# Bulk transfers issued from ScalarE's queue, projection inputs prepared one tile further ahead, and a last output tile made in two column halves

## The reference

```python
for l in range(2):                      # W_stack[l]: 512 x 1024
    proj = x @ W_stack[l]
    Wh, Ws = jnp.split(proj, 2, axis=-1)
    a = jax.nn.softmax(Wh @ Ws.T, axis=-1) * adj
    x = jax.nn.leaky_relu(a @ Wh + x, 0.01)
# then, on the normalised x:
xw = jnp.maximum(jnp.sign(x), 0.0) @ jnp.sign(weight).T
x = layernorm(x + jax.nn.relu(adj @ xw))
```

## Time and profile before

| | us |
|---|---|
| runs: median of 3 (lowest, highest) | 2148.17 (2147.42, 2153.5) |
| profiled execution, its own time | 2151.31 |
| its span | 2149.4 |
| PE busy | 2110.1 (98%) |
| DVE busy | 1592.3 (74%) |
| ACT busy | 908.2 (42%) |
| POOL busy | 689.5 (32%) |
| DMA queue q1 (SP's): share of 16 engines | 73.8% |
| DMA queue q10 (ACT's): share of 16 engines | 1.8% |

### The profile page before, as it was taken

One profiled execution on the slowest core, in us unless ns is written; L12 is line 12 of the kernel. 1 busy time (PEld: TensorE's weight loads), 2 busy tenths in 40 slices (PEclk: granted clock), 3 DMA queues, 4 the chain that ended last, 5 costly groups with the idle time before them and its releaser, 6 DMA issues.

```text
span 2149.4 us, 38691 instructions
## 1 busy us (share of the span) xinstructions
PE 2110.1 (98%) x13260; PEld 1295.3 (60%) x13260; DVE 1592.3 (74%) x4057; ACT 908.2 (42%) x2047; POOL 689.5 (32%) x623
## 2 busy tenths in 40 slices
PE   6999999999999999999999999999999999999998
PEld 2456666666666666664446666666666666665444
DVE  7987877788877778876986776776677776767465
ACT  5764344444444444443765344344434443443000
POOL 2853223232223233222863232333323332322000
PEclk9999999999999999999999999999999999999999
DMA  7998878788878687769998987888878978779794
GB/s 216 213 222 155 175 154 164 157 155 161 169 151 166 154 165 159 161 138 236 204 211 183 184 162 165 162 167 172 168 155 171 169 161 181 158 157 220 218 304 133
DMA packets 779526, 380.18 MB, mean 177 GB/s; under 512 B 642880, under 2 KB 701376, under 8 KB 777664
## 3 DMA queue, kind: packets, MB, share of 16 engines
q1 hardware_dynamic: 768512, 341.89, 73.8%
q0 software_dynamic: 3328, 22.16, 7.0%
q10 hardware_dynamic: 7488, 13.63, 1.8%
HBM read 206.24 MB, written 59.11 MB: 123 GB/s over the span
## 4 chain that ended last, share of the span: by engine, by line
PE 91%; DVE 3%; DMA 2%; issue 1%; ACT 1%; SPq 1%; POOL 0%; DVEq 0%; ACTq 0%; POOLq 0%
PE banks L1157 38%; PE banks L1126 31%; PE banks L783 10%; PE banks L1661 7%; PE banks L1135 3%; DMA adj_rows_a<-adj_rows 1%; PE banks L1115 1%; PE banks L605 1%; DVE halves_a L1385 1%; DMA values<-x_rows 0%; DMA probs_t_a<-halves_a 0%; DVE row_a L1340 0%; SPq L1002 0%; DVE adj_low L1453 0%; DVE w_p L725 0%
## 5 line engine op out<-in xcount | busy, mean ns | idle before, releaser
L1157 PE MATMUL banks<-values,probs_t_a 128*128 128x512 f16 x4056 | 961.2, 380 | 7.3 <-DMA probs_t_a<-halves_a 4.2
L1323 POOL TENSOR_TENSOR row_a<-row_a,adj_rows_a 128x512 f32<-128x512 f32 (+1 forms) x364 | 456.7, 1269 | 1163.7 <-ACT row_a L1245 1133.6
L1157 PEld LDWEIGHTS banks<-values,probs_t_a 128*128 128x128 f16 x4056 | 397.3, 98 | 382.2 <-issue 9.6
L1237 ACT ACTIVATE row_a<-banks 128x256 f32<-128x256 f32 x468 | 177.3, 379 | 628.6 <-PE banks L1126 609.1
L1126 PE MATMUL banks<-keys_t,q_even_a 128*128 128x256 f16 x3528 | 430.9, 273 | 1.8 <-DVE peaks_a L1340 1.1
L1385 DVE SCALAR_TENSOR_TENSOR halves_a<-row_a,halves_a 128x512 f16<-128x512 f32 (+1 forms) x364 | 272.5, 749 | 192.1 <-ACT halves_a L1260 189.7
L1126 PEld LDWEIGHTS banks<-keys_t,q_even_a 128*128 128x128 f16 x3528 | 343.8, 98 | 102.5 <-DVE peaks_a L1340 4.9
L1126 PE MATMUL banks<-keys_t,q_odd_a 128*128 128x256 f16 x3024 | 370.0, 273 | 4.4 <-DVE peaks_a L1340 1.8
L1245 ACT ACTIVATE row_a<-row_a,shift_a,scales 128x512 f32<-128x512 f32 (+1 forms) x364 | 281.4, 774 | 174.0 <-DVE shift_a L1375 173.9
L1126 PEld LDWEIGHTS banks<-keys_t,q_odd_a 128*128 128x128 f16 x3024 | 294.3, 98 | 92.1 <-DVE peaks_a L1340 6.0
L1407 DVE SCALAR_TENSOR_TENSOR acc_a<-acc_a,factor_a,banks 128x512 f32<-128x512 f32 x312 | 232.8, 746 | 106.1 <-PE banks L1157 99.3
(11 more groups left out here) (131 smaller groups left out, 1482.7 us busy)
## 6 DMA issues: line engine op xcount, KB each, us to landing
adj_rows_a<-adj_rows SPq DMA_DIRECT2D x312, 256.0 KB, 3.2
adj_t<-adj_blocks POOLq DMA_DIRECT2D x104, 208.0 KB, 3.9
keys_t<-adj_t SPq DMA_DIRECT2D x26, 832.0 KB, 7.9
x_rows_a<-x_rows SPq DMA_DIRECT2D x52, 256.0 KB, 3.6
s_rows<-sum_rows_p SPq DMA_DIRECT2D x24, 512.0 KB, 3.1
values<-x_rows SPq DMA_DIRECT2D x13, 512.0 KB, 5.4
adj_rows_a<-adj_rows SPq DMA_DIRECT2D x52, 128.0 KB, 2.7
x_mid<-x_rows_a SPq DMA_DIRECT2D x26, 256.0 KB, 3.4
```

What stands on the lines that cost most here:

```text
L1157: last = pe.matmul(out_bank(u), probs_t[:, turned_slot(w), u, ph * tiles + j, :], values[:, 4 * step_of(w) + j, vh, :], start=(j == 0 and ...
L1237: act.activation(quarter(w, u, odd), as_quarter(bank(w, SET_A)), ACT.Copy).then_inc(scores_copied, 1)
L1323: pool.tensor_tensor(piece, piece, adj_rows[:, n % ADJ_RING, 0:width(w)], ALU.mult).then_inc(masked, 1)
```

## The change

It has four parts.

1. **Bulk loads change their queue.** `load_x` for layer 1's rows (not its last), the two small transfers for the weights' peak, `gather_low_bits`, the 22 loads of products and the first 8 loads of adjacency tiles are issued by ACT, at the end of its iteration w, where SP issued them at the end of its own.
2. **Five tiles are prepared ahead, not four** (`FILL = 5`). In layer 0 the fifth tile's high half is made after the last squares and its low half inside `scale_layer`; at the layer seam the five high halves are spread over five iterations.
3. **Layer 0's start is put in another order**: ACT takes the squares of tiles 2 and 3 (DVE did), and makes tile 2's high half between the two sides of the weights.
4. **The last output tile** is made in two column halves of 256: 2 x 26 matmuls into two banks, the first half measured while PE makes the second, the output made and stored in two halves, the second by SP.

```diff
-RING, X_RING = 4, 3
+RING, X_RING, FILL = 4, 3, 5
@@ scale_layer(dve)
         dve.reduce_max(facts[:, 5:6], norms2[:], AX_X).then_inc(norm_peak, 1)
+        if layer == 0:
+            x_lo_half(dve, 4)
         dve.wait_ge(norm_all, layer + 1)
@@ project: act_program
             x_hi_half(act, 1)
+            square_rows(2)
+            square_rows(3)
             act.wait_ge(w_scale_ready, layer + 1)
             for side in (0, 1):
                 for c in range(DC):
                     halve_w(c, cols_of(side))
-            x_hi_half(act, 2)
+                if side == 0:
+                    x_hi_half(act, 2)
...
             for t in range(FIRST + 2, T, 2):
                 square_rows(t)
+            x_hi_half(act, 4)
...
-                if 2 * i + RING + two < T:
-                    x_hi_half(act, 2 * i + RING + two)
+                if 2 * i + FILL + two < T:
+                    x_hi_half(act, 2 * i + FILL + two)
@@ attend: sp_program
-            if ahead and piece_windows.get(w - 3, -1) == pieces - 1:
-                ahead["send_w_peak"](sp)
...
-                ending = w - (windows - STEPS)
-                if 2 <= ending < 5:
-                    binary["load_products"](sp, ending - 2)
-                elif ending in (5, 6, 12, 13):
-                    n = (5, 6, 12, 13).index(ending)
-                    binary["load_adj16"](sp, 2 * n)
-                    binary["load_adj16"](sp, 2 * n + 1)
...
-                if 0 <= behind < WIDE:
-                    ahead["load_x"](sp, 2 * behind)
-                    ahead["load_x"](sp, 2 * behind + 1)
@@ attend: act_program, at the end of an iteration
-            if ahead and w == windows:
-                for t in range(RING):
-                    ahead["x_hi_half"](act, t)
+            if ahead and 0 <= w - windows < FILL:
+                ahead["x_hi_half"](act, w - windows)
+            behind = w - (windows - STEPS) - LAG - 1
+            if ahead and 0 <= behind < WIDE:
+                ahead["load_x"](act, 2 * behind)
+                ahead["load_x"](act, 2 * behind + 1)
...
+            ending = w - (windows - STEPS)
+            if last_layer and 2 <= ending < 5:
+                binary["load_products"](act, ending - 2)
+            elif last_layer and ending in (5, 6, 12, 13):
+                n = (5, 6, 12, 13).index(ending)
+                binary["load_adj16"](act, 2 * n)
+                binary["load_adj16"](act, 2 * n + 1)
@@ binary layer: finish_end(t, b), for the last tile
+            for side, summed, count in ((0, half_summed, 1), (1, sums_done, t + 1)):
+                dve.wait_ge(summed, count)
+                links.link(dve.scalar_tensor_tensor(out=work[:, b, parts[side]], in0=end_bank(t, side), scalar=0.0,
+                                                    in1=work[:, b, parts[side]], op0=ALU.max, op1=ALU.add))
+                links.link(dve.bn_stats(end_stats[:, side], work[:, b, parts[side]]))
...
+            for side, done in ((0, end_half_done), (1, rows_done)):
+                dve.tensor_scalar(y_rows[:, b, parts[side]], work[:, b, parts[side]], stats[:, b, 6:7], std[:, b, 2:3],
+                                  ALU.subtract, ALU.mult).then_inc(done, 1)
```

More of the change, by code:

```diff
@@ L1094, in sp_program @@
                     store(t)
[L1095 to L1096 removed]
+                if 0 <= w - windows < RING:
                     ahead["turn_x"](sp, w - windows)
[L1098 to L1100 removed]
     def sign_bank(t):
@@ L1744, in finish_tile @@
             stores = 16 * done // 2
-            chain.tile(done + t)
+            chain.tile(done + t - (1 if done else 0))
             dve.wait_ge(y_loaded[b], landed(t, b) + stores)
@@ L1778, in dve_program @@
         dve.wait_ge(rstd_made, 1)
-        for t in range(T):
+        for t in range(T - 1):
             finish_tile(t, t % 2, out_bank(t), 0)
+        finish_end(T - 1, (T - 1) % 2)
         if_low_bits(dve, split_tiles)
```

69 lines of the change are left out of this document (48 added, 21 removed).

## The result

The changed kernel takes 2170.18 us (median of 6 runs, 2167.26 to 2179.84), the kernel before 2150.35 beside it: a ratio of 1.0098 [1.0076, 1.012] (in brackets, here and below, the 95% interval). It is 20 us slower. I had forecast 2140.8 with 2135 to 2151 as the range, and 0.06 for slower. The profiled execution is the fastest of the six: its own time is 2167.26, its span 2165.5, that is 16.1 us over the span before.

A forecast was written before the change was run, and what follows sets the result against it. PE, busy for 98% of the span, was taken as the bound. Seam -3.4, end of layer 1 -5.2, start +1.9 and tail -0.7 sum to -7.4 us; applied to the median 2148.17 this gives 2140.8, range 2135 to 2151.

The forecast's parts named there:

- the delay sits in the issue and order of one queue: Seam and end of layer 1: turns' issues took 2.08 and 5.21 us in SP's queue; bulk loads on ACT would relieve them.
- Seam, -3.4 predicted: Between the layers: PE's 3.0 us wait falls to 0.6, its 1.6 us low clock goes, 0.6 given back; bounds -4.6 and 0.
- Nothing won: Between the layers: the bound where the last `adj` piece still takes 6.35 us to land, at 987.9.
- End of layer 1, -5.2 predicted: Last windows: PE's waits for turned probabilities go but for 0.4 us, with 1.6 us of low clock; bounds -5.8 and +1.
- Products, 0 predicted: End of three windows: ACT's 22 product loads at 0.64 us each fit its 4.17 us wait; shows beyond 0.69 us an issue.
- rival D: ACT held by its own load issues: PE waits from 0.76 us an issue, slower from 1.1, 2168 at 2.0; chance 0.08.
- Start, +1.9 predicted: Layer 0: `evict` net +0.3 us, and PE stands 3.7 us before tile 6 with 1.6 us of low clock; bounds -1 and +2.8.
- Tail, -0.7 predicted: Behind the last matmul: DVE -0.55 us, PE +0.1, output 0 to 0.3 later, half-size store -0.6 to 0; bounds -1.1 and -0.1.

## Why the prediction was wrong

**The step that failed** is the one at the seam and again at the end: "the delay sits in the issue and order of one queue", so that a bulk load in another queue lets piece and turn land in 4.5 and 3.7 us. I read the order of SP's queue as the cause of the delay. It was also what paced the loads: SP could issue them only behind a window's second turn, at 967.0, 978.4 and 987.6, where ACT alone with them issued at 962.9, 972.7 and 982.4, 4 to 6 us sooner. On ACT they go out 0.4 us ahead of the turns, and turns of 5.7 to 8.9 us follow. Shown: by the pair of kernels that swap moment and queue, and by the turn measured alone (6.4 us against 6.1).

**Seam, -3.4 predicted.** Measured alone: +8.2 us, 1.0038. I had named the moment ("two bulk loads that ACT issues at about 980.4") and taken 4.5 us for a landing between 2.7 and 6.35; it was 6.8, beyond the bound. Nor was the piece issued 0.9 us earlier: it went out 5.9 us behind the start of the last score block (988.53), where it had been 3.75 (982.42). "Nothing won" was no bound, because the moment moved too. The prize was also over-read: the 3.0 us wait and its 1.6 us of low clock belong to an execution whose seam took 21.75 us, where seven others with that code took 18.79 to 19.69, with waits of 1.16 to 1.84 us and no low clock. With all of the delay removed the seam became 1 to 1.5 us shorter.

**End of layer 1, -5.2 predicted.** The diagnosis was right: the tiles stand ahead of the last two turns, and with that undone 5.4 us come (0.25% of 2150). The means was wrong. On ACT the tiles run beside the turns, which take 8.5 us in place of 3.7, and PE waits 4.13 us for `acc_a` instead, with a PEclk of 0.50 behind it.

**Products, 0 predicted.** I wrote that the cost would show beyond 0.69 us an issue; it was 0.88 in the first window (7 in 6.18 us) and 0.71 and 0.76 in the others. The measured price is 0.2 to 3.9 us. That is rival D's mechanism at a small price: D said a wait from 0.76 on, and PE waited 1.53 us behind 0.88. It is not what made the kernel 20 us slower.

**Start, +1.9 predicted.** Right in mechanism and size: alone 3.7 us [1.7, 5.6]; in the four kernels with the fifth tile the stage is 1.7 to 2.7 us over the median of 148.18 of the others. PE's wait before tile 6 was 2.9 to 3.5 us (3.7 predicted) with a PEclk of 0.50 behind it. What I had not seen is that the low clock also falls there without the fifth tile: in 3 of the 12 other kernels with the old start this stage took 149.75 us or more, and 149.55 in the one with the new order and four tiles. The price is thus partly a matter of how often the low clock falls there, and one execution of each kernel can't tell that.

**Tail, -0.7 predicted.** DVE saved 0.3 us as worked out (0.55 less 0.3), PE paid 0.2. The failed term is the store: half the bytes were to give 0 to -0.6, and SP's store gave +1.5. I took a duration seen on one queue for another.

**Interaction.** 0.38, 0.27, 0.17 and 0.09% add up to 0.91% of the 0.98: the parts explain the whole within their intervals. In the one execution read, though, the changed kernel's seam took 30.53 us, 6 us over the 24.47 with the row loads alone on ACT. What its timeline has beyond that kernel's is this: with the five high halves spread, ACT issues the fourth and fifth pair of row loads at 996.4 to 1000.9, ahead of the first turn of a projected tile (1001.93, landed after 11.1 us); with the halves made at once ACT was held until that turn had landed. This I read from the two timelines; it was not tried by itself.

## What to carry to other kernels

Before you move a transfer to another queue, ask when the new issuer gets to it: an order that looks like a delay may be the pacing that keeps bulk loads away from short, urgent ones. To free a turn, place the bulk behind it in the same queue (one number here: 0.9975) before trying a second queue. And read a wait of a few us in several executions before you count it as the prize, above all where the stage ahead of it varies.

## What the runs showed of the hardware

- A transposing transfer of 128 x 1024 16-bit elements lands 3.0 us after its issue, 5.2 behind two 512 KB loads of its own queue, and 6.4 beside the same loads in the other; a plain 128 KB piece 2.0, 4.0 and 2.8. Only the plain one profits from a second queue.
- The turn's loss beside the other queue's loads depends on the distance within about 2 us: 3.4, 5.0, 6.4 and 3.2 us for loads 2.2 and 1.1 us ahead, together, and 1.0 behind.
- The last store from SP, otherwise idle, took 2.9 to 3.9 us to land with 128 KB; ACT's of the same size 1.8 to 1.9. Why is open; it wasn't tried with the queues swapped.
- A wait of PE of 2.0 to 2.9 us was followed by the low clock in some executions and not in others: behind 2.02 us at 41.7 the 48 matmuls took 10.53 us in one kernel and 12.22 in another with the same wait (12.22 behind 2.03 in the kernel before).
